# Layer two of a two-layer encoder: a unit's weighted values in two pieces, one behind each of its score blocks

## What is computed

```python
def _L1_xattn_ref(queries, keys, values, W_q, b_q, W_k, b_k, W_v, b_v, W_o, b_o):
    ...
    scores = jnp.einsum('bhqd,bhkd->bhqk', Q, K) / jnp.sqrt(jnp.asarray(d, Q.dtype))
    attn = jax.nn.softmax(scores, axis=-1)
    out = jnp.einsum('bhqk,bhkd->bhqd', attn, V)
    ...
    return out @ W_o.T + b_o
...
x = x + _L0_xattn_ref(_layernorm(x, axis=-1), fside_BxSxS_0, ctx_1024, ctx_1024, ...)
x = x + _L0_ffn_ref(_layernorm(x, axis=-1), ...)
x = x + _L1_xattn_ref(_layernorm(x, axis=-1), ctx_1024, ctx_1024, ...)
x = x + _L1_ffn_ref(_layernorm(x, axis=-1), ...)
```

## Time and profile before

| | us |
|---|---|
| median of 3 runs | 1438.31 |
| lowest, highest | 1438.08, 1440.24 |
| the profiled execution's own time | 1436.72 |
| its span | 1434.9 |
| granted TensorE clock, mean | 0.956 |
| TensorE busy (matmuls) | 1271.0 (89%) |
| VectorE busy | 1083.2 (75%) |
| ScalarE busy | 828.7 (58%) |
| GpSimd busy | 875.1 (61%) |

### The profile page before, as it was taken

The page is one execution under the profiler, slowest core; times in us unless marked ns, Lnnn a source line. Parts: engine busy times, 40 slices in busy tenths (PEclk is TensorE's granted clock), DMA queues, the critical chain, the costliest instruction groups (busy, mean ns, idle before and its releaser), DMA issues. The chain is left out here.

```text
span 1434.9 us, 44416 instructions
## 1 busy us (share of the span) xinstructions
PE 1271.0 (89%) x16309; PEld 1052.2 (73%) x16309; DVE 1083.2 (75%) x3396; ACT 828.7 (58%) x1582; POOL 875.1 (61%) x947
## 2 busy tenths in 40 slices
PE   1789999999999999279999999669999999869997
PEld 0367787777777787279999999437777778746775
DVE  6778999989988896547766666458888888736663
ACT  1167777767777767156666666235666666534452
POOL 5346888888888856547777777544555544136650
PEclk9799999999999999689999999879999999979999
DMA  5676677777777760535555554588888887445765
GB/s 167 220 220 212 216 248 245 235 225 251 240 233 225 219 193 30 194 53 64 65 65 65 64 65 63 103 235 224 265 271 268 260 264 234 127 104 120 178 166 131
DMA packets 212422, 252.15 MB, mean 176 GB/s; under 512 B 38256, under 2 KB 173680, under 8 KB 205040
## 3 DMA queue, kind: packets, MB, share of 16 engines
q1 hardware_dynamic: 179552, 226.33, 52.7%
q0 software_dynamic: 25840, 21.71, 10.8%
q10 hardware_dynamic: 6816, 1.29, 0.5%
HBM read 156.73 MB, written 91.46 MB: 173 GB/s over the span
## 5 line engine op out<-in xcount | busy, mean ns | idle before, releaser
L822 DVE TENSOR_REDUCE L_neg_max<-L_ps_mx 128x2 f32<-128x496 f32 (+1 forms) x768 | 489.1, 660 | 93.4 <-PE L_ps_mx L1006 90.7
L674 ACT ACTIVATE L_p<-L_ps_sc 120x512 f32<-120x512 f32 (+1 forms) x768 | 417.3, 598 | 207.5 <-PE L_ps_sc L993 203.9
L1006 PE MATMUL L_ps_mx<-stack_k,stack_q 118*128 118x248 bf16 (+1 forms) x2048 | 299.7, 251 | 45.8 <-DMA stack_q<-L_q_rows 29.9
L993 PE MATMUL L_ps_sc<-stack_q,stack_k 122*120 122x128 bf16 (+1 forms) x3072 | 300.3, 222 | 5.0 <-DMA stack_q<-L_mT 2.4
L993 PEld LDWEIGHTS L_ps_sc<-stack_q,stack_k 122*120 122x120 bf16 (+1 forms) x3072 | 239.3, 123 | 58.2 <-issue 34.4
L1507 POOL DMA_INDIRECT routed_out<-M_y,M_x x135 | 211.9, 1570 | 88.5 <-DVE M_y L1598 87.3
L1030 PE MATMUL L_ps_o<-L_p,L_v 120*18 120x128 f32 (+1 forms) x6144 | 219.7, 275 | 3.3 <-ACT L_o_sb L703 2.9
L1006 PEld LDWEIGHTS L_ps_mx<-stack_k,stack_q 118*128 118x128 bf16 x2048 | 141.9, 100 | 106.7 <-issue 36.5
L1030 PEld LDWEIGHTS L_ps_o<-L_p,L_v 120*18 120x18 f32 (+1 forms) x6144 | 147.3, 98 | 38.1 <-issue 24.8
L1377 POOL DMA_INDIRECT routed_in<-R_xn,R_slot x128 | 127.1, 993 | 42.5 <-issue 35.9
L1553 ACT COPY M_w<-stack_k 128x768 f32 x135 | 112.1, 832 | 53.9 <-PE M_ps_g L1530 36.9
(11 more groups left out here) (210 smaller groups left out, 2127.3 us busy)
## 6 DMA issues: line engine op xcount, KB each, us to landing
L_q_rows<-L_q_parts_sb SPq DMA_DIRECT2D x192, 192.0 KB, 4.1
stack_q<-L_q_rows SPq DMA_DIRECT2D x192, 192.0 KB
stack_k<-L_k_rows SPq DMA_DIRECT2D x96, 372.0 KB
stack_k<-L_k_rows SPq DMA_DIRECT2D x96, 180.0 KB
F_spread<-F_gate_rows SPq DMA_DIRECT2D x32, 512.0 KB, 6.5
L_k_rows<-L_k_parts_sb SPq DMA_DIRECT2D x32, 372.0 KB, 4.2
M_x<-routed_in SPq DMA_DIRECT2D x135, 66.0 KB, 2.0
L_k_rows<-L_k_parts_sb SPq DMA_DIRECT2D x32, 180.0 KB, 4.2
```

Source lines behind the costliest of these rows:

```text
L674: nc.scalar.activation(p_t[t][u % 2][:, quarter * 4 * S:(quarter + 1) * 4 * S], ps_sc[n % NSC][0:KEYS[t], :], ACT.Exp).then_inc(sc_read, 1)
L822: nc.vector.tensor_reduce(neg_max[:, b, kk * HPB:(kk + 1) * HPB], v, AX.X, ALU.max, negate=True).then_inc(max_read, 1)
L993: last = mm(ps_sc[n % NSC][0:KEYS[t], j * S:(j + 1) * S], k_st[p][:, b // 2, h, b % 2, k0:k0 + KEYS[t]], q_st[p][:, b // 2, h, b % 2], sta ...
L1006: last = mm(ps_mx[i % NMX][:, j * NK:(j + 1) * NK], q_st[p][0:TERM_TOP, b // 2, h, b % 2], k_st[p][0:TERM_TOP, b // 2, h, b % 2], start=Tr ...
```

## The change

In `UNIT` of layer two the entry `("values", 0)` moves from behind `("scores", 1)` to behind `("scores", 0)`; `("values", 1)` stays behind `("scores", 1)`. Layer one's list is not touched.

```diff
     else:
         UNIT = [
-            ("job", 0), ("scores", 0), ("max", 0), ("scores", 1), ("values", 0), ("values", 1), ("job", 1),
+            ("job", 0), ("scores", 0), ("values", 0), ("max", 0), ("scores", 1), ("values", 1), ("job", 1),
             ("max", 1),]
```

## The result

The changed kernel took 1460.35 us, median of 4 runs (1457.93 to 1471.99), against 1439.28 for the kernel before (4 runs, 1438.08 to 1441.78). The ratio is 1.016, with a 95% interval from 1.0103 to 1.0217: slower, by about 21 us. The forecast was 1463.0, range 1451 to 1473. The profiled execution took 1457.93 us with a span of 1456.2, 21.3 more than before.

The account below looks back on a forecast made before the run. TensorE, its matmuls busy 97% of layer two's steady stretch, was taken to bound; 26.7 + 7 - 9 = +24.7 us on 1438.31 gave 1463.0 us, with 1451 to 1473 expected to hold 8 times in 10.

Parts of the forecast that it names:

- What bounds: Layer two's steady stretch: TensorE, matmuls busy 97% at clock 1.00, bounds; VectorE and ScalarE wait for it.
- Step 1: Layer two's values on TensorE: one more way in and out per divided burst, 127 x 0.21 = +26.7 us.
- Step 2: First values in units 1 and 5: longer waits for the copy of the values' bank, +7 us (0 to +14).
- Step 3: TensorE's waits for `attT` and transfers, and first-group switches: swallowed or hidden by longer units, -9 us (0 to -13).
- the division is free: First half to max tile: way in and out free or nearly so, kernel 6 us faster, 1432; chance 0.04.
- The chain: Copy waits delay max tile, second scores, then ScalarE's exponentials: about +42 us, +58 at worst; chance 0.08.
- The clock: Layer two: TensorE's granted clock falls to the lower level for a tenth of 285 us, +28 more; chance 0.03.
- the two rules: Burst boundary: next weights pulled ahead and drain hidden, about -2 in all, against tiling-mode change draining TensorE; rows favoured the latter.
- spacing is worth nothing here: Layer two's max tiles 0.88 and 0.88 us apart instead of 1.10 and 0.44: no gain, no TensorE wait on `L_neg_max`.

Follow-up runs that it names:

- The narrow small matmul: Kernel before plus, in each layer-two unit between first scores and first max tile, one 32-column bf16 matmul with 64 columns of weights: 1.0114 of the kernel before.
- The run on the other chip: The changed kernel, unedited, against the kernel before, both on another chip: ratio 1.011 (1.0076 to 1.0144).
- the wide matmul: Kernel before plus, in each layer-two unit between first scores and first max tile, one 32-column bf16 matmul with 128 columns of weights: 1.001 of the kernel before.

## Why the prediction was right

**What bounds.** Right: a dearer boundary on TensorE in layer two came out as a longer layer two, and nothing else moved.

**Step 1, +26.7, measured +29.3.** The kind and the mechanism hold, the size was a little low. Start to start, half a burst takes 0.346 and the whole one 0.565, so the second way out costs 2 x 0.346 - 0.565 = 0.127; scores to values instead of to the max tile is 0.319 - 0.226 = 0.093; and max tile to scores is 0.221 where it was 0.212 directly behind a burst, 0.009 that I had not seen. Together 0.229 us, times 127 is 29.1. I had read 0.22 and rounded down to 0.21. The starts inside a burst say the same in another way: its groups of four matmuls follow each other by 0.11 to 0.12 us (1051.038, 1051.159, 1051.269 and 1051.377 in the burst of rows 4), and the last is followed by the max tile after 0.226, 0.12 more. The narrow small matmul shows that this is the price of the shape and not of the values.

**Step 2, +7, measured +5.5.** The places were right, 15 in unit 5 and 7 in unit 1. In unit 5 the wait was 0.17, not 0.28, or 2.6 us instead of 4.5: the copy now starts 0.92 us after the second scores (1056.51 to 1057.43), where it was 1.02. In unit 1 it was 0.93 in 4 groups and 0.45 to 0.67 in 3, and here the reading of the rows was off. Of the five waits before, four stand in unit 1 and not three (0.62, 0.72, 0.42 and 0.68 from start to start; the fifth is the last group's in unit 5). Three of these grew to 0.93, by 0.31, 0.21 and 0.51 for the forecast's 0.25, and the last group's stayed. Of the three groups that had not waited, one waits 0.93 and two 0.45, for the forecast's 0.6.

**Step 3, -9, measured -12.9.** The sum was too small in each of its terms, and the list was not complete. From start to start, `L_attT` gave back 3.9 us (forecast 3.6), the maxima's and the context's transfer 4.5 (3.5), the first group some 2.4 (1.7); nothing of the first two is left. The rest, some 2 us, lies mostly in scores behind OP and VP and in the router's jobs at the end, which the prediction did not name. The run on the other chip had 2.6 us less of waits in all where this one has 7.4 (12.9 less, 5.5 more), so this term is the least certain, as its bounds said. That the forecast of the whole came so near is in part luck: on the two chips the waits alone differ by 5 us.

**The sum.** 26.7 + 7 - 9 = 24.7 against 29.3 + 5.5 - 12.9 = 21.9. The three errors (+2.6, -1.5, -3.9) partly cancel. The prediction called itself wrong altogether if layer two were not longer by 20 us; it passed that line by 2.

**The rivals.** That the division is free is excluded: work by the account rose by 29.3 and 28.0 us on two chips, and the loader's places of 0.2 us ahead of max tiles rose from 99 to 212. The chain did not come: the longest wait for the copy is 0.93. The clock stayed at 1.00 in the windows of layer two. The weighing of the two rules came out as the rows had it. The Trainium skill's page "TensorEngine Tiling (Array Packing)", section "Key Properties", says that a change of tiling mode drains TensorE. The runs agree as far as the price goes: the next start comes 0.03 us after the wide matmul and 0.13 after the narrow one; that it is a drain, they don't show. The Trainium skill's page "TensorE: Matmul & The Clock Gate", section "Step-by-step: what each phase is for", with the next weights pulled ahead and one drain under the next fill, fits the full-width neighbours, where the extra 32 columns add 0.03 us, and not the boundary of a narrow piece.

**What I would not have got right.** The prediction said that spacing is worth nothing here, since no wait on max tiles showed. For this change that was true. As a statement on the kernel it was not: moving whole bursts cost 16 us in layer two, through the copy and a transfer, and 28 and 46 in layer one, through waits on max tiles.

## What to carry to other kernels

In this kernel a few matmuls on part of the array's columns among full-width ones cost about 0.1 us to enter and 0.12 to leave, for 1, 8, 16 and 32 counted matmuls, in fp32 and in bf16; so count the bursts, keep them whole, and read the price as the difference between bursts of two lengths from start to start. When such a price is added or taken away, take it against the waits of the same engine: a third of an added 26 us vanished in them, and 14 us saved were given back whole in waits that are mostly for VectorE, which was busy for 0.87 of the stretch already. And a piece's place has a price of its own if two other engines take what stands around it from two or three buffers: ask what moves away from it as well as what it moves towards.

## What the runs showed of the hardware

A single bf16 matmul of 32 columns costs 0.03 us with 128 columns of weights and 0.23 to 0.24 with 64, all boundaries counted. Going from fp32 strips of 32 columns to a bf16 matmul of 64 costs as much as going to the full width: 0.34 us behind half a burst. Scores that stand directly behind a narrow piece take 0.27 us to their successor where others take 0.22, and a max tile directly behind one takes 0.21 and not more; I had not looked for that before, and why it differs wasn't tried. The kernel before took 1564 us on one chip and about 1440 on the others. A kernel of that chip's set whose layer one is untouched had a granted clock of 0.89 between 100 and 500 us, where the others have 1.00, and 625 us instead of 503 in layer one; what slowed that chip wasn't looked into.
